# Next weights turned by VectorE in 32x32 blocks, loads that exchange partition groups, and a contraction index dealt with a stride of four

## The chip, the cores and the metric

The kernel runs on one core of one Trainium2 chip. The metric is the device time of one execution in microseconds (us); three runs of the kernel before have a median of 3421.34 us (3419.98 to 3421.66). The engines are TensorE (PE; its weight loads are listed as PEld), VectorE (DVE), ScalarE (ACT), GpSimd (POOL) and SyncE (SP, which here only issues DMAs).

## The reference

All tensors are f32; 128 sequences of 32 tokens with 512 channels (4096 tokens).

1. Conditional mixing: a small MLP on `cond_128` gives each sequence a 32x32 matrix and a bias, with which its 32 rows are mixed.
2. A Mamba-like block of 8 groups: `proj = h @ in_proj_w.T` (in_proj_w has 10304 rows of 512), a causal convolution of 4 taps with SiLU, a scan per head (`state = state*dA + dt*x*B; y = state.C`), a norm per group of 512 channels, a gate, and `out = yn @ out_proj_w.T` (out_proj_w is 512 x 4096). It is added to x.
3. A grouped convolution and a 512x512 layer whose weights are decoded from bit planes with a table of 16 or 256 entries per output row; the wide table serves rows of large norm. It is added too.

What matters for the change is only how in_proj_w and out_proj_w get into the form that TensorE wants: contraction index on the partitions, and each weight as a high part (rounded to the matmul's format) and a low part (the rest), since each f32 product is made of three passes (high.high, high.low, low.high).

## The kernel before, in words

Stage 1 (until about 113 us) makes the mixed rows h for 8 blocks of 512 tokens and stores them, high and low, in `h_d`, and turns the 14 weight chunks (128x512 each) of group 0: `turn` transposes a chunk in four 128x128 pieces on TensorE, ScalarE copies the high part from PSUM, VectorE subtracts for the low part. `mix_chunk` takes 128 columns of x (`xb`) as stationary operand for each k of the four contraction pieces.

Stage 2 is a loop over 8 groups g and, within one, 8 blocks j; `attend` is its body on every engine, run 64 times. In groups 0 to 6 it is called with `prepare`: it also prepares two chunks of the next group's weights. One body does, on TensorE in this order: six projections (`project`, 12 matmuls each, L1119) for B, C and four of x; C.B products (L1156); the decay sums (L1164); three gate projections; the transposes of xc (`turn_x`, L1126); eight 128x128 transposes of the next weights (L1181) into two banks; the scan (L1136), whose first part waits tile by tile for `dtx`; the fourth gate projection; the output product (L1211). Without `prepare` (last group) there are no such transposes and the third gate projection comes after `turn_x`.

VectorE does in this order: the convolutions (L1343) with pieces of the wide-table decode between them, four scan matrices `m` (L1361), four products `dtx` (L1368, these need `turn_x`), two low parts of the next weights (L1381, these need ScalarE's copy), then `y`, `z`, the low parts of `gy`, squares, more of the decode, and the addition to `acc` (L1438). ScalarE does the first taps (L1252), SiLU (L1234), the exponentials (L1258), gates 0 to 2 (`gate`, L1238), the two high copies of the next weights (L1269), then high parts of `gy` and squares with gate 3 between them. GpSimd makes the scan's products and the root.

SyncE issues in each body, in this order (`step`): a wait until the residual of the body before is stored, the loads of the two raw chunks (`load_raw`, one DMA of 256 KB each), the residual's load, in the last block of a group the reloads of `wt` as its projections come free, the stores of the two prepared chunks, the next h, and the residual's store. A group has 16 chunk places: place u = 0 takes the convolution and gate chunks 2 + j, place u = 1 takes chunks 0 and 1 in turn in blocks 0 to 3 and the four chunks of out_proj in blocks 4 to 7. Order between engines is by semaphores only, written out by hand.

Stage 3 (from about 3141 us) is the last layer. It isn't touched.

Of the kernel before, what the change touches and what calls it, by code (L numbers as in the profile page):

```python
# [18 lines left out]
F32 = mybir.dt.float32  # L19
# [4 lines left out]
ACT = mybir.ActivationFunctionType  # L24
# [3 lines left out]
P = 128  # L28
# [90 lines left out]
def same_line(nc, sb, name, partner):  # L119

    gap = (partner - next_place(nc)) % LINE
    if gap:
        sb(name, [P, gap // 4])


# [9 lines left out]
def mix_part(nc, a, sh, ctx):  # L135
# [98 lines left out]
    def block_at(place):  # L234

        return (place + 1) % NBLK

    def raw_chunk(n):

        if n < NPJ_ALL:  # L240
            return raw[n][:, :]
        return sh.stage[n - NPJ_ALL][:, :]
# [131 lines left out]
    def tensor_part(pe):  # L374

        def turn(n):

            pe.wait_ge(s_rawin[n], 16)
            if TURN_AFTER[n]:
                if TURN_AFTER[n] > NPJ_ALL:  # L380
                    pe.wait_ge(sh.s_wot, 16 * (TURN_AFTER[n] - NPJ_ALL))
                else:
                    pe.wait_ge(sh.s_wt[TURN_AFTER[n] - 1], 16)
            for k in range(KC):
                ins = pe.transpose(sh.bank[TURN[n]][:, k * P:(k + 1) * P], raw_chunk(n)[:, k * P:(k + 1) * P], sh.ident[:, :])
            ins.then_inc(s_wps, 1)
# [50 lines left out]
        def mix_chunk(j, k, alone=False):  # L437

            for t in range(TT):
                ins = pe.matmul(p_h[k][:, t * P:(t + 1) * P], xb[j % 2][:, t, k * P:(k + 1) * P], mix[:, TT * block_at(j) + t, :],  # L440
                                start=(alone and t == 0), stop=(not alone and t == TT - 1), skip_group_check=True)
            if not alone:
                ins.then_inc(s_hp, 1)
# [37 lines left out]
        for k in range(KC):  # L481
            ins = pe.transpose(p_wdt[:, k * H:(k + 1) * H], wdt[:, k * P:(k + 1) * P], sh.ident[0:H, 0:H])
        ins.then_inc(s_pe, 1)
# [372 lines left out]
def attend_part(nc, a, sh, ctx):  # L856
# [39 lines left out]
    bank = sh.bank  # L896
    XT, SEG, CB, YB, OUT, SSQ, NEXT = (3, 4, 5, 7), (5, 7), 6, (6, 7, 4, 5), (2, 3, 4, 5), 6, (0, 1)

    s_raw = [sem(f"s2_raw{u}") for u in range(2)]
    s_nps = sem("s2_nps")
    s_nhi = sem("s2_nhi")
# [69 lines left out]
    def sync_part(sp):  # L973
# [9 lines left out]
        def load_raw(g, j):  # L983
            for u, n in enumerate(next_chunks(j)):
                sp.dma_start(stage[u][:, :], weight_rows(a, n, g)).then_inc(s_raw[u], 16)

# [123 lines left out]
    def tensor_part(pe):  # L1110
        def attend(g, j, prepare):
# [50 lines left out]
            for q in range(SEGB):  # L1162
# [4 lines left out]
                ins.then_inc(s_seg, 1)  # L1167
            for c in range(CT - 1 if prepare else CT - 2):
                pe.wait_ge(s_conv, NCV * it + 4 + c)
                project(NCV + c)  # L1170
# [5 lines left out]

            for u in range(2 if prepare else 0):
                pe.wait_ge(s_raw[u], 16 * it + 16)
                pe.wait_ge(s_z, CT * it + CT + 1 + u)
                for k in range(KC):  # L1180
                    ins = pe.transpose(bank[NEXT[u]][:, k * P:(k + 1) * P], stage[u][:, k * P:(k + 1) * P], sh.ident[:, :])  # L1181
                ins.then_inc(s_nps, 1)
            if not prepare:
                pe.wait_ge(s_conv, NCV * it + NCV)
                project(NCV + CT - 2)
            pe.wait_ge(s_cbm, it + 1)
# [3 lines left out]
            pe.wait_ge(s_z, CT * it + CT + 1)  # L1190
            if prepare:
                pe.wait_ge(s_nlo, 2 * it + 1)
            project(NCV + CT - 1)

            pe.wait_ge(s_z, CT * it + CT + 3)
            if prepare:
                pe.wait_ge(s_nlo, 2 * it + 2)
            for c in range(CT):
# [29 lines left out]
    def scalar_part(act):  # L1228
        def attend(g, j, prepare, first=False):
# [36 lines left out]
            for u in range(2 if prepare else 0):  # L1266
                act.wait_ge(s_nps, 2 * it + u + 1)
                act.wait_ge(s_nst, 32 * it + 32)
                act.activation(wnext[:, u, 0, :], bank[NEXT[u]][:, :], ACT.Copy).then_inc(s_nhi, 1)  # L1269
            high(0)  # L1270
# [19 lines left out]
    def vector_part(dve):  # L1290
        lut8 = sh.lut8[:, :, :].rearrange("p t c -> p (t c)").bitcast(I32)
        la, lb, lc, ld = (x[:, :] for x in leaf)
        def attend(wt_tile, gl, j, prepare, first=False):
            g = G // OT * wt_tile + gl
# [79 lines left out]
            for t in range(TT):  # L1374
                scan_matrix(t)
            for t in range(TT):
                times_dt(t)

            for u in range(2 if prepare else 0):
                dve.wait_ge(s_nhi, 2 * it + u + 1)  # L1380
                dve.tensor_tensor(wnext[:, u, 1, :], bank[NEXT[u]][:, :], wnext[:, u, 0, :].bitcast(F32),  # L1381
                                  ALU.subtract).then_inc(s_nlo, 1)
# [57 lines left out]

        with dve.Fori(0, NBLK) as j:
            attend(0, 0, j, True, first=True)
        with dve.Fori(0, NBLK) as j:
            attend(0, 1, j, True)
        for wt_tile in range(1, OT):
            with dve.Fori(0, G // OT - (wt_tile == OT - 1)) as gl:
                with dve.Fori(0, NBLK) as j:
                    attend(wt_tile, gl, j, True)
        with dve.Fori(0, NBLK) as j:
# [444 lines left out]
```

## Time and profile before

| | us |
|---|---|
| median of three runs | 3421.34 |
| the profiled execution's own time | 3419.63 |
| its span, first to last instruction | 3417.9 |
| PE busy | 3395.8 |
| DVE busy | 3025.9 |
| ACT busy | 1406.9 |
| POOL busy | 446.0 |
| mean granted TensorE clock | 0.999 |

Busy time is the time in which at least one instruction of the engine is under way; waits, semaphore work and DMA issues aren't in it. The queues' mean busy share of the 16 DMA engines is 38.8%. The time of a kernel is taken from its own runs; the profile is one execution, whose length differs a little.

### The profile page before, as it was taken

How to read it: one execution, taken by the hardware profiler on the slowest of the kernel's cores; microseconds unless marked ns; L12 is line 12 of the kernel's file. 1: busy time of each engine (PE TensorE's matmuls, PEld its weight loads, DVE VectorE, ACT ScalarE, POOL GpSimd, SP SyncE). 2: the span in 40 equal slices, each digit the busy share in tenths (PEclk: the TensorE clock that was granted, in tenths of full speed). 3: DMA queues.
4: the chain of work that ended last, by engine and by line, in shares of the span. 5: the costliest groups of instructions: out<-in, count | busy, mean ns of one | idle time of the engine just before them, and what ended most of it. 6: DMA issues, size and time to landing. Idle time of an engine off the chain costs nothing. (4 is left out here: it accounts for less than half of the span.)

```text
span 3417.9 us, 58378 instructions
## 1 busy us (share of the span) xinstructions
PE 3395.8 (99%) x19738; PEld 2869.8 (84%) x19738; DVE 3025.9 (89%) x4815; ACT 1406.9 (41%) x2179; POOL 446.0 (13%) x328
## 2 busy tenths in 40 slices
PE   8999999999999999999999999999999999999999
PEld 6788888888888888888888888888888888888888
DVE  6899999999999999999999999999999999998443
ACT  5555553444434444344443444434444334433111
POOL 1111111011110111101111011110111100111333
PEclk9999999999999999999999999999999999999999
DMA  7433263234432353325433262335423352225331
GB/s 270 172 117 123 105 226 132 107 135 161 159 130 109 135 191 128 131 108 191 136 128 132 107 221 106 127 132 181 148 106 127 131 181 94 76 95 154 93 92 59
DMA packets 207789, 466.23 MB, mean 136 GB/s; under 512 B 35134, under 2 KB 80606, under 8 KB 198284
## 3 DMA queue, kind: packets, MB, share of 16 engines
q1 hardware_dynamic: 206364, 464.72, 38.8%
q0 software_dynamic: 368, 0.85, 0.1%
q10 hardware_dynamic: 1024, 0.27, 0.0%
q8 instruction: 15, 0.25, 0.0%
q14 instruction: 18, 0.15, 0.0%
HBM read 313.68 MB, written 152.09 MB: 136 GB/s over the span
## 5 line engine op out<-in xcount | busy, mean ns | idle before, releaser
L1119 PE MATMUL p_cv<-ht,wt 128*128 128x512 f32 x5376 | 1274.5, 392 | 0.8 <-DVE xc L1343 0.8
L1119 PEld LDWEIGHTS p_cv<-ht,wt 128*128 128x128 f32 x5376 | 1004.0, 188 | 224.3 <-issue 11.0
L1211 PE MATMUL bank<-wot,gy 128*128 128x512 f32 x3072 | 728.3, 392 | 0.0
L1211 PEld LDWEIGHTS bank<-wot,gy 128*128 128x128 f32 x3072 | 571.9, 188 | 121.0
L1252 ACT ACTIVATE xc<-p_cv,cvb,cvw 128x512 f32<-128x512 f32 x256 | 200.0, 782 | 898.6 <-PE p_cv L1119 898.4
L1343 DVE SCALAR_TENSOR_TENSOR xc<-p_cv,cvw,xc 128x496 f32<-128x496 f32 (+2 forms) x768 | 545.0, 717 | 22.1 <-ACT xc L1252 0.2
L1119 PE MATMUL bank<-ht,wt 128*128 128x512 f32 x2304 | 554.6, 390 | 0.0
L1119 PEld LDWEIGHTS bank<-ht,wt 128*128 128x128 f32 x2304 | 431.9, 188 | 89.3
L1071 POOL TENSOR_TENSOR r<-rv,neg_half 128x4 f32<-128x4 f32 x64 | 89.5, 1398 | 2345.0 <-DVE rv L1423 2345.0
L1065 POOL TENSOR_TENSOR segr<-adts,mask_le 128x1024 fp32r<-128x1024 f32 x128 | 243.0, 1920 | 424.0 <-DVE adts L1326 424.0
L1361 DVE TENSOR_TENSOR m<-cbm,y 128x1024 f32<-128x1024 f32 x256 | 295.9, 1218 | 0.0
L1343 DVE SCALAR_TENSOR_TENSOR xc<-bank,cvw,xc 128x496 f32<-128x496 f32 (+2 forms) x384 | 274.5, 715 | 11.2 <-ACT xc L1252 2.2
L1234 ACT ACTIVATE xc<-xc 128x512 f32<-128x512 f32 x384 | 234.5, 627 | 65.2 <-DVE xc L1343 64.0
L1242 ACT ACTIVATE gy<-z 128x512 fp32r<-128x512 f32 x256 | 161.3, 630 | 212.2 <-DVE z L1397 212.2
L1136 PE MATMUL bank<-m,dtx 128*64 128x128 f32 x4096 | 237.7, 274 | 0.0
L1136 PEld LDWEIGHTS bank<-m,dtx 128*64 128x64 f32 x4096 | 222.3, 137 | 12.2 <-issue 12.2
L1368 DVE TENSOR_TENSOR dtx<-bank,dt_all 128x512 f32<-128x512 f32 x256 | 160.4, 684 | 74.3 <-PE bank L1126 74.3
L1397 DVE SCALAR_TENSOR_TENSOR z<-z,nw,y 128x512 f32<-128x512 f32 x256 | 192.4, 752 | 29.8 <-DVE y L1393 5.7
L1393 DVE SCALAR_TENSOR_TENSOR y<-xc,dsk,bank 128x512 f32<-128x512 f32 x256 | 189.6, 741 | 10.4 <-PE bank L1136 10.4
L1685 PE MATMUL p_y<-wq,x3t 128*128 128x512 f32 x768 | 182.9, 394 | 0.0
L1386 DVE TENSOR_TENSOR gy<-z,gy 128x512 fp32r<-128x512 f32 x256 | 175.2, 684 | 0.0
L1438 DVE SCALAR_TENSOR_TENSOR acc<-bank,r,acc 128x512 f32<-128x512 f32 x256 | 173.6, 740 | 0.0
(191 smaller groups left out, 3418.1 us busy)
## 6 DMA issues: line engine op xcount, KB each, us to landing
ht<-h_d SPq DMA_DIRECT2D x63, 2048.0 KB, 7.9
acc_d<-acc SPq DMA_DIRECT2D x64, 1024.0 KB, 4.3
wt_d<-wnext SPq DMA_DIRECT2D x112, 512.0 KB, 3.4
acc<-acc_d SPq DMA_DIRECT2D x56, 1024.0 KB, 7.1
wt<-wt_d SPq DMA_DIRECT2D x70, 512.0 KB, 8.4
stage<-in_L_attn_in_proj_w SPq DMA_DIRECT2D x84, 256.0 KB, 2.8
wot<-wt_d SPq DMA_DIRECT2D x28, 512.0 KB, 6.4
xb<-in_x SPq DMA_DIRECT2D x8, 1024.0 KB, 8.3
```

The lines of the kernel that those rows point to most:

```text
L1065: pool.tensor_tensor(segr[:, half, :, :], adts[:, half, :].bitcast(F32).unsqueeze(2).to_broadcast([P, TT * HG, L]), sh.mask_le[:, :].unsqu ...
L1119: ins = pe.matmul(pb[:, :], wt[:, n, l, k, :], ht[:, rr, k, :], start=(q == 0 and k == 0), stop=(q == 2 and k == KC - 1))
L1136: ins = pe.matmul(bank[YB[c]][u * HP:(u + 1) * HP, t * P:(t + 1) * P], dtx[:, t, h * HP:(h + 1) * HP], m[:, h, t, :], start=True, stop=True)
L1211: ins = pe.matmul(bank[OUT[t]][:, :], gy[:, c, l, t * P:(t + 1) * P], wot[:, rr, c, :], start=(c == 0 and q == 0), stop=(c == CT - 1 and q ...
L1234: act.activation(xc[:, n, :], xc[:, n, :], ACT.Silu).then_inc(s_silu, 1)
L1252: act.activation(xc[:, n, :], bank[PROJ_BANK[n]][:, :], ACT.Identity, bias=cvb[:, n:n + 1], scale=cvw[:, n, TAPS - 1:TAPS]).then_inc(s_tap, 1)
L1343: ins = dve.scalar_tensor_tensor(dst, src, cvw[:, n, TAPS - 1 - k:TAPS - k], dst, ALU.mult, ALU.add)
L1361: dve.tensor_tensor(m[:, :, t, :].rearrange("p h (c l) -> p h c l", l=L), cbm[:, t, :].rearrange("p (c l) -> p c l", l=L).unsqueeze(1).to_ ...
L1386: dve.tensor_tensor(gy[:, c, 1, :], z[:, c, :], gy[:, c, 0, :].bitcast(F32), ALU.subtract).then_inc(s_ulo, 1)
L1393: dve.scalar_tensor_tensor(y[:, c, :], xc[:, 2 + c, :], dsk[:, c:c + 1], bank[YB[c]][:, :], ALU.mult, ALU.add).then_inc(s_y, 1)
L1397: dve.scalar_tensor_tensor(z[:, c, :], z[:, c, :], nw[:, c:c + 1], y[:, c, :], ALU.mult, ALU.mult).then_inc(s_u, 1)
L1685: ins = pe.matmul(p_y[t % 2][q][:, :], x3t[:, l, t, r, :], wq[:, q, rr, r, :], start=(n == 0 and r == 0), stop=(n == 2 and r == R - 1))
```

## The change

Three parts, which need each other.

1. In stage 2 the next weights are no longer transposed by TensorE. VectorE's `transpose` turns 32x32 blocks each in its place; the exchange of the blocks themselves is done by the loads, which put each square of 32 rows on another group of 32 partitions. A chunk of in_proj is loaded by four DMAs (pieces of 512 bytes), a chunk of out_proj by sixteen (pieces of 128 bytes), the last four of them behind a wait for the first twelve. VectorE's transpose stands after the scan matrices and ahead of `dtx` and writes to where the low part will be; ScalarE's high copy and VectorE's low part then read it from SBUF.
2. For in_proj the contraction index is dealt with a stride of four: piece k holds channels k, k+4, k+8, ... in place of 128 neighbours, so the block transpose reads every fourth word of its source. The first group's weights, x in `mix_chunk` and the dt weights follow (`inner_columns`). The chunks of out_proj keep their order; for them the source is read without a step, and since that is another instruction, VectorE's loops over j are cut into blocks 0 to 3 and 4 to 7.
3. TensorE's order with `prepare` becomes the one without: two gate projections, `turn_x`, the third, the scan, the fourth; its waits for the low parts of the next weights go.

```diff
+def inner_columns(src, k):
+    return src.rearrange("p (q c) -> p c q", c=KC)[:, k, :]
...
             for k in range(KC):
-                ins = pe.transpose(sh.bank[TURN[n]][:, k * P:(k + 1) * P], raw_chunk(n)[:, k * P:(k + 1) * P], sh.ident[:, :])
+                columns = inner_columns(raw_chunk(n), k) if n < NPJ_ALL else raw_chunk(n)[:, k * P:(k + 1) * P]
+                ins = pe.transpose(sh.bank[TURN[n]][:, k * P:(k + 1) * P], columns, sh.ident[:, :])
...
-                ins = pe.matmul(p_h[k][:, t * P:(t + 1) * P], xb[j % 2][:, t, k * P:(k + 1) * P], mix[:, TT * block_at(j) + t, :],
+                ins = pe.matmul(p_h[k][:, t * P:(t + 1) * P], inner_columns(xb[j % 2][:, t, :], k), mix[:, TT * block_at(j) + t, :],
...
-            ins = pe.transpose(p_wdt[:, k * H:(k + 1) * H], wdt[:, k * P:(k + 1) * P], sh.ident[0:H, 0:H])
+            ins = pe.transpose(p_wdt[:, k * H:(k + 1) * H], inner_columns(wdt[:, :], k), sh.ident[0:H, 0:H])
...
         def load_raw(g, j):
             for u, n in enumerate(next_chunks(j)):
-                sp.dma_start(stage[u][:, :], weight_rows(a, n, g)).then_inc(s_raw[u], 16)
+                src = weight_rows(a, n, g)
+                for m in range(P // L):
+                    if n < NPJ:
+                        sp.dma_start(stage[u][m * L:(m + 1) * L, :].rearrange("p (m x) -> p m x", x=P),
+                                     src[:, m * P:(m + 1) * P].rearrange("(m p) x -> p m x", p=L)).then_inc(s_raw[u], 16)
+                        continue
+                    parts = src[m * L:(m + 1) * L, :].rearrange("p (c b e) -> b p c e", c=KC, e=L)
+                    if m == P // L - 1:
+                        sp.wait_ge(s_rawout, 16 * (P // L - 1) * (P // L) * (KC * (g - 1) + j - (NBLK - KC) + 1))
+                    for b in range(P // L):
+                        sp.dma_start(stage[u][b * L:(b + 1) * L, m * P:(m + 1) * P].rearrange("p (c e) -> p c e", e=L),
+                                     parts[b]).then_inc(s_rawout if m < P // L - 1 else s_raw[u], 16)
...
-            for c in range(CT - 1 if prepare else CT - 2):
+            for c in range(CT - 2):
                 pe.wait_ge(s_conv, NCV * it + 4 + c)
                 project(NCV + c)
...
-            for u in range(2 if prepare else 0):
-                pe.wait_ge(s_raw[u], 16 * it + 16)
-                pe.wait_ge(s_z, CT * it + CT + 1 + u)
-                for k in range(KC):
-                    ins = pe.transpose(bank[NEXT[u]][:, k * P:(k + 1) * P], stage[u][:, k * P:(k + 1) * P], sh.ident[:, :])
-                ins.then_inc(s_nps, 1)
-            if not prepare:
-                pe.wait_ge(s_conv, NCV * it + NCV)
-                project(NCV + CT - 2)
+            project(NCV + CT - 2)
...
             pe.wait_ge(s_z, CT * it + CT + 1)
-            if prepare:
-                pe.wait_ge(s_nlo, 2 * it + 1)
             project(NCV + CT - 1)
             pe.wait_ge(s_z, CT * it + CT + 3)
-            if prepare:
-                pe.wait_ge(s_nlo, 2 * it + 2)
...
                 act.wait_ge(s_nps, 2 * it + u + 1)
-                act.wait_ge(s_nst, 32 * it + 32)
-                act.activation(wnext[:, u, 0, :], bank[NEXT[u]][:, :], ACT.Copy).then_inc(s_nhi, 1)
+                act.activation(wnext[:, u, 0, :], wnext[:, u, 1, :].bitcast(F32), ACT.Copy).then_inc(s_nhi, 1)
...
+            if prepare:
+                dve.wait_ge(s_nst, 32 * it + 32)
+            for u in range(2 if prepare else 0):
+                dve.wait_ge(s_raw[u], 16 * (P // L) * it + 16 * (P // L))
+                dve.transpose(wnext[:, u, 1, :].bitcast(F32).rearrange("p (k m e) -> p m k e", k=KC, e=L),
+                              stage[u][:, :].rearrange("p (m k e) -> p m k e" if u == 1 and out_rows else "p (m e k) -> p m k e",
+                                                       k=KC, e=L)).then_inc(s_nps, 1)
             for t in range(TT):
                 times_dt(t)
...
-                dve.tensor_tensor(wnext[:, u, 1, :], bank[NEXT[u]][:, :], wnext[:, u, 0, :].bitcast(F32),
+                dve.tensor_tensor(wnext[:, u, 1, :], wnext[:, u, 1, :].bitcast(F32), wnext[:, u, 0, :].bitcast(F32),
                                   ALU.subtract).then_inc(s_nlo, 1)
...
+        HALVES = ((0, NBLK - KC, False), (NBLK - KC, NBLK, True))
+        for lo, hi, out_rows in HALVES:
+            with dve.Fori(lo, hi) as j:
+                attend(0, 0, j, True, first=True, out_rows=out_rows)
...
```

## Rows read from the trace of the kernel before

**Rows 1.** The page, part 1: busy us (share of the span) xinstructions.

```profile
PE 3395.8 (99%) x19738; PEld 2869.8 (84%) x19738; DVE 3025.9 (89%) x4815; ACT 1406.9 (41%) x2179; POOL 446.0 (13%) x328
```

**Rows 2.** Windows over one body of group 3 and one of the last group.

```profile
1502.16:1549.61 47.45, 47.45 (x278) 40.14 (x276) 44.48 (x71) 19.75 (x31) 5.22 (x3) 1.00 0.34 120
3016.69:3063.27 46.58, 46.58 (x269) 39.16 (x268) 43.27 (x69) 18.55 (x29) 5.20 (x3) 1.00 0.24 90
```

**Rows 3.** Waits: who waited for whom, us in total, times, longest.

```profile
DVE dtx L1368 <- PE bank L1126: 74.3, 56, 1.3
...
DVE z L1397 <- DVE y L1393: 5.7, 24, 0.5
```

**Rows 4.** Timeline of TensorE, bodies as in rows 2: start, length, what.

```profile
1509.43 2.89 PE L1119 MATMUL bank<-ht,wt 128*128 128x512 f32 x12
...
1513.90 1.04 PE L1181 MATMUL p_cv<-ident,stage 128*128 128x128 f32 x8
1514.86 3.71 PE L1136 MATMUL bank<-m,dtx 128*64 128x128 f32 x64
...
1533.24 5.65 PE L1119 MATMUL p_cv<-ht,wt 128*128 128x512 f32 x24
...
3023.97 1.91 PE L1126 MATMUL bank<-ident,xc 128*128 128x128 f32 x16
```

**Rows 5.** Timeline of VectorE in the body of group 3.

```profile
1506.83 4.63 DVE L1361 TENSOR_TENSOR m<-cbm,y 128x1024 f32<-128x1024 f32 x4
1512.79 2.53 DVE L1368 TENSOR_TENSOR dtx<-bank,dt_all 128x512 f32<-128x512 f32 x4 [1.33 <-PE bank L1126]
1515.25 1.29 DVE L1381 TENSOR_TENSOR wnext<-p_cv,wnext 128x512 fp32r<-128x512 f32 x2
1516.45 0.74 DVE L1393 SCALAR_TENSOR_TENSOR y<-xc,dsk,bank 128x512 f32<-128x512 f32 x1
```

**Rows 6.** Timeline of ScalarE in the same two bodies.

```profile
1506.85 1.16 ACT L1234 ACTIVATE xc<-xc 128x512 f32<-128x512 f32 x2
...
1514.62 1.09 ACT L1269 ACTIVATE wnext<-p_cv 128x512 fp32r<-128x512 f32 x2 [1.67 <-PE p_cv L1181]
...
3028.64 0.60 ACT L1238 ACTIVATE z<-bank 128x512 f32<-128x512 f32 x1 [3.88 <-PE bank L1119]
```

**Rows 7.** Groups of instructions (busy us, mean ns of one), and a timeline row of L730.

```profile
L730 DVE STREAM_TRANSPOSE turned<-p_cv 128x512 f32<-128x512 f32 x2 | 1.3, 694 | 1.9 <-PE p_cv L420 1.9
L687 DVE TENSOR_SCALAR bits<-bits 128x512 int32<-128x512 int32 x3 | 1.1, 422 | 0.0
...
18.15 1.31 DVE L730 STREAM_TRANSPOSE turned<-p_cv 128x512 f32<-128x512 f32 x2 [1.87 <-PE p_cv L420]
```

**Rows 8.** Groups with strided operands, one plain load (L1126), and the mix timeline.

```profile
L261 DVE COPY mix<-turned 32x256 f32<-32x256 f32 x4 | 1.5, 378 | 0.1
L270 ACT ACTIVATE mix<-turned 32x256 f32<-32x256 f32 x4 | 2.6, 653 | 4.9 <-DVE turned L730 4.9
L1279 ACT ACTIVATE acc<-z 128x512 f32<-128x512 f32 x32 | 33.6, 1126 | 42.7 <-DMA z<-in_x 42.7
L1753 DVE TENSOR_REDUCE sqs<-sq 128x128 f32<-128x512 f32 x32 | 34.9, 1091 | 40.6 <-ACT sq L1713 40.6
L1126 PEld LDWEIGHTS bank<-ident,xc 128*128 128x128 f32 x1024 | 115.6, 140 | 8.4
L1662 PEld LDWEIGHTS p_y<-ident,w 128*128 128x128 f32 x12 | 1.7, 209 | 0.2 <-DVE wq L1736 0.2
...
90.37 2.05 PE L440 MATMUL p_cv<-mix,xb 128*128 128x128 f32 x16
```

**Rows 9.** SyncE's timeline; the landing of L1596's loads; an issue row (KB, landing).

```profile
1542.06 0.35 SPq L985 DMA_DIRECT2D stage<-in_L_attn_in_proj_w  x1
...
3168.89 4.49 SPq L1596 DMA_DIRECT2D x2p<-acc_d  x8
...
DMA to landing us min/median/max: 2.4/3.2/4.2
...
cvw<-in_L_attn_conv_weight SPq DMA_DIRECT2D x8, 8.0 KB, 2.9
```

More of the change, by code:

```diff
@@ L896, in attend_part @@
     bank = sh.bank
-    XT, SEG, CB, YB, OUT, SSQ, NEXT = (3, 4, 5, 7), (5, 7), 6, (6, 7, 4, 5), (2, 3, 4, 5), 6, (0, 1)
+    XT, SEG, CB, YB, OUT, SSQ = (3, 4, 5, 7), (5, 7), 6, (6, 7, 4, 5), (2, 3, 4, 5), 6
     s_raw = [sem(f"s2_raw{u}") for u in range(2)]
+    s_rawout = sem("s2_raw_out_parts")
     s_nps = sem("s2_nps")
@@ L1292, in vector_part, with attend @@
         la, lb, lc, ld = (x[:, :] for x in leaf)
-        def attend(wt_tile, gl, j, prepare, first=False):
+        def attend(wt_tile, gl, j, prepare, first=False, out_rows=False):
             g = G // OT * wt_tile + gl
@@ L1439, in attend @@
                                          ALU.mult, ALU.add).then_inc(s_acc, 1)
[L1441 to L1444, printed above, removed]
+        HALVES = ((0, NBLK - KC, False), (NBLK - KC, NBLK, True))
+        for lo, hi, out_rows in HALVES:
+            with dve.Fori(lo, hi) as j:
+                attend(0, 0, j, True, first=True, out_rows=out_rows)
+        for lo, hi, out_rows in HALVES:
+            with dve.Fori(lo, hi) as j:
+                attend(0, 1, j, True, out_rows=out_rows)
         for wt_tile in range(1, OT):
             with dve.Fori(0, G // OT - (wt_tile == OT - 1)) as gl:
-                with dve.Fori(0, NBLK) as j:
-                    attend(wt_tile, gl, j, True)
+                for lo, hi, out_rows in HALVES:
+                    with dve.Fori(lo, hi) as j:
+                        attend(wt_tile, gl, j, True, out_rows=out_rows)
         with dve.Fori(0, NBLK) as j:
```

## The prediction

> **What bounds the kernel now.** I read the page first: TensorE (PE) is busy 99% of the span, VectorE 89% [rows 1]. Most of the span is one body run 64 times (8 groups of 8 blocks), so next I cut one body out of the middle by windows: 47.45 us with `prepare`, in which PE is busy for all 47.45; one of the last group, without `prepare`, takes 46.58, again with PE busy throughout, and the granted clock is 1.00 in both [rows 2]. The sums of busy time understate VectorE, because its short gaps between dependent instructions count as idle, so I read the waits instead: in the 56 prepared bodies VectorE waits for another engine in one place only, 74.3/56 = 1.33 us before the `dtx` products, for TensorE's transposes of xc [rows 3]. VectorE's own loop is then 47.45 - 1.33 = 46.12 us. So TensorE is the bound, and VectorE is 1.33 us behind it; whatever VectorE gets beyond that is on the path.
>
> **The change, step by step.**
>
> *TensorE loses the eight transposes of the next weights.* They start at 1513.90 and the scan follows at 1514.86: 0.96 us [rows 4]. What is left, order included (transposes of xc ahead of the third gate projection), is the stream that the last group runs already. Its 46.58 us is the new floor of TensorE: 0.87 less. If nothing else held, 56 x 0.87 = 49 us would go. The last group also shows that the new order is harmless to PE: the transposes of xc need the last silu, which ends at 1506.85 + 1.16 = 1508.01, and PE would reach them at 1509.43 [rows 4, 6].
>
> *VectorE gains two 32x32-block transposes of 128x512 per body,* ahead of `dtx`. The one transpose in the trace, twice 128x512 from PSUM in stage 1, takes 694 ns, and the two together 1.31, so the second starts 0.62 after the first [rows 7]. The new ones read SBUF, which makes no difference: the scan matrices, all from SBUF, run 4 x 1024 elements in 4.63, 1.13 ns each, and a low part that reads PSUM has a pitch of 0.60 for 512 (the instruction after the pair starts 1.20 after the first, by the chain of [rows 5]: 1515.25 to 1516.45), 1.17 ns each. But 84 of the 112 read with a step of four words (16 bytes), which no VectorE row shows. Bounds: below, a 1-input instruction of the same size at 422 ns (pitch 0.34 by the same overlap) [rows 7]; above, the strided sum over `sq` at 1091 ns (pitch 1.02). ScalarE's strided copy `acc<-z`, with exactly this step of 16 bytes, is at 1126 ns [rows 8] where its plain copy takes 0.60 [rows 6], so a strided read can cost 1.9 times. The nearest row for VectorE is a copy whose read steps 128 bytes: 256 elements in 378 ns, while ScalarE takes 653 for the same kind of copy of the same size [rows 8]. 378 ns is about one element per cycle of 1.04 ns plus 0.11, no worse than its unit-step instructions; the `sq` row is a reduction over runs of four, which may be slow for that alone. I take 0.62 for each transpose, strided or not.
> The row `acc<-z` shows ScalarE paying for a 16-byte step. The Trainium skill, "SBUF — State Buffer", section "Door 1: The DMA port swizzle", says that SBUF delivers in lines of 16 bytes and wants at least two hits per line for full rate; taken at its word, a step of four f32 has one hit, and the strided transposes cost what the first rival below says. The VectorE copy in rows 8 speaks against it for this engine.
>
> *What the cover is worth.* VectorE ends the scan matrices at 1506.83 + 4.63 = 1511.46 and idles until 1512.79 [rows 5]. Now it transposes there (from 1511.39, since an instruction overlaps the one before by 0.07), and the transposes of xc, 2.7 us earlier on PE, are done before it gets to `dtx`. New loop of VectorE: 46.12 + 2 x 0.62 = 47.36 us, above PE's 46.58. The wait on TensorE is gone; what is late next is VectorE itself, and TensorE waits for it (at the scan, for the fourth `dtx`, about 0.8 us). Net: 47.36 - 47.45 = -0.09 per body, 56 x -0.09 = **-5.0 us**.
>
> *ScalarE's high copy and VectorE's low part* keep their count and size. The copy now stands behind the third gate, whose projection moved behind the transposes of xc. In the last group this gate starts 3028.64 - 3023.97 = 4.67 after those transposes start [rows 4, 6]. With them at 1509.43 or 0.16 earlier (`dtx` can start at 1511.39 + 1.24 = 1512.63 in place of 1512.79, and PE's lead comes from there) the gate starts near 1514.0, the copies (a pair spans 1.09: pitch 0.49, length 0.60) end near 1515.1 and 1515.6. VectorE wants its low parts at 1511.39 + 1.24 + 4 x 0.61 = 1515.1 and 1515.7. It fits with about 0.1 to spare: I charge 0 and keep up to 0.3 per body for the range. Queued behind a late low part are the `y`, `z` and square steps, so it would be on the bound's path.
>
> *SyncE's loads.* Two issues per body become 8 in blocks 0 to 3 and 20, with a wait for twelve landings in the middle, in blocks 4 to 7. The first issue is at 1542.06, once the residual is stored [rows 9]. Eight issues to a quarter of the partitions, with register work, take 4.49, 0.56 each, and such a load lands in 3.2 us (2.4 to 4.2) [rows 9]. In the long case the sixteenth is issued at 1542.06 + 15 x 0.56 = 1550.5, lands at 1553.6, the last four are out at 1555.3 and land at 1558.5. VectorE wants chunk 0 at 1511.39 + 47.36 = 1558.75 and chunk 1, the one loaded so, at 1559.4. Margin 0.9 us: cost 0, up to 1 us in each of 28 bodies if both landings are at the 4.2 end. Behind them in the queue stand the residual's load, some 12 us later then and wanted only at the block's end, and in the last block of a group nine reloads of `wt`, which go out from about 1556 on and are wanted one after the other from the next block's start, 25 us later (1533.24 + 47.45 = 1580.7, by the first projection of the block shown) [rows 4]. The store of the prepared weights and the load of ht follow events of the compute engines later than that. Cost 0. DMA traffic: same bytes, pieces of 512 or 128 bytes; 512 pieces of 16 bytes (8 KB of `cvw`) land in 2.9 us [rows 9].
>
> *VectorE's loops are cut in halves.* One more loop start for each of 7 group passes. The trace's few starts of a gap that belong to no engine (`z` behind `y`, 5.7 us in 24 cases, 0.5 at most) [rows 3] bound it: 0 to 4, I take +1.
>
> *Stage 1 reads x and the first weights with the step of four.* 256 matmuls of `mix` and 44 transposes load strided operands. Plain transposes load in 140 ns, those of stage 3 with this very step in 209 [rows 8]. Loads overlap the matmuls: 16 of `mix` take 2.05, 0.128 each [rows 8], less than one plain load, so most of the 69 ns should hide. Bounds 0 and 256 x 0.069 = 18 us; I take +1.
>
> **Sum:** -5.0 + 1 + 1 = -3 us on the profiled execution's 3419.63. The median of the runs is 1.7 above that, 3421.34, so the time to forecast is **3418 us**. What a measurement here can tell from no change is 0.2%, 6.8 us; this is within it.
>
> **Rivals.**
> 1. *VectorE pays for the 16-byte step* (the other side). Place: the 84 strided transposes, pitch 1.02 in place of 0.62. Blocks 0 to 3: 46.12 + 2.04 = 48.16, +0.71 x 28 = 19.9; blocks 4 to 7, where chunk 1 of out_proj is read plainly: 46.12 + 1.64 = 47.76, +0.31 x 28 = 8.7. With the +2 above: 3421.3 + 30.6 = 3452. It decides from a mean pitch of 0.665 per transpose on (1.33/2). For: ScalarE, PE loads and the reduction in rows 8. Against: the VectorE copy there.
> 2. *The high copy comes late,* 0.3 us per body: loop 47.66, +0.21 x 56 = 12, time 3421.3 + 12 + 2 = 3435. For: the margin of 0.1; against: PE has 0.8 us of slack to run ahead.
> 3. *The raw rows come late in blocks 4 to 7,* by 1 us: +28 - 3, time 3446. Against: the margin of 0.9. The Trainium skill, "DMA: Bandwidth & Descriptors", "Specifications", wants 512 bytes per piece for line rate, with a read-modify-write below; at that the 128-byte pieces would be this rival. The row of 16-byte pieces speaks for a landing of about 3 us all the same.
> 4. *Transposes are cheap,* pitch 0.34: loop 46.80, -0.65 x 56 + 2 = -34, time 3387. For: 422 ns for a 1-input instruction; against: 694 ns for the transpose itself.
> 5. *PE's lost work is not what held it* (a reload or the clock takes its place) and nothing moves: 3421. Against: no wait of PE in the bodies.
>
> **How the numbers follow.** Forecast 0.61, rival 1 0.17, rival 2 0.08, rival 3 0.05, rival 4 0.05, rival 5 0.04. The forecast's own range, with a pitch of 0.59 to 0.66 and the +2 between 0 and 8, is 3412 to 3428: of its 0.61 I give 0.17 to faster than 3414.5, 0.39 to within, 0.05 to slower than 3428. Faster 0.17 + 0.05 = 0.22. Same 0.39 + 0.04 + 0.01 (a mild rival 2) = 0.44. Slower 0.05 + 0.17 + 0.07 + 0.05 = 0.34. The range goes from 3409 to 3452: it leaves out rival 4, the forecast's tail below and half of rival 1.
>
> **What would show it.** Body period 47.3 to 47.4 in groups 0 to 6 and 46.58 in the last. STREAM_TRANSPOSE in the body at 0.69 us in both patterns; 1.09 in the strided one means rival 1. No wait before `dtx`; PE idle 0.8 per body before the scan for `dtx`. A VectorE wait before `wnext` for ACT means rival 2, one before the transpose for DMA of `stage` rival 3. LDWEIGHTS of `mix` near 0.21, stage 1 ending within 2 us of before. I am wrong at the root if VectorE has waits left in the body while PE is idle: then a loop over two engines sets the period, which I haven't summed.

## The result and the profile after

| | before | after |
|---|---|---|
| median, us (four runs each) | 3421.15 | 3456.93 |
| lowest to highest | 3419.98 to 3421.66 | 3456.59 to 3457.55 |
| span of the profiled execution | 3417.9 | 3455.8 |

After takes 1.0105 times as long as before [1.0088, 1.0123]: slower by 1%, 39 us above the 3418 forecast and 5 above the end of the range.

The page of after, part 1 (columns as in rows 1):

```profile
PE 3415.6 (99%) x19290; PEld 2844.2 (82%) x19290; DVE 3113.7 (90%) x4927; ACT 1404.7 (41%) x2179; POOL 445.5 (13%) x328
```

PE issues 448 matmuls fewer (8 in each of 56 bodies) and is busy 20 us longer. The matmuls of `mix` alone are busy 64.4 us, 36.8 before; and a matmul that is held up counts as busy: the scan's 4096 matmuls, unchanged, are busy 270.1 us (L1154), 237.7 before (L1136). As in [rows 1], 99% doesn't say that PE's own work is what takes the time.

I laid the spans side by side at one mark of each body, the start of VectorE's product for C.B. The first such mark stands at 127.13 us before and 150.47 after; from there the distances from mark to mark are:

| | before | after | count | together, us |
|---|---|---|---|---|
| until the first mark | 127.13 | 150.47 | 1 | +23.3 |
| blocks 0 to 3, groups 0 to 6 | 47.46 | 47.77 | 28 | +8.7 |
| blocks 4 to 7, groups 0 to 6 | 47.46 | 47.41 | 28 | -1.4 |
| on top, one body between two groups (54.33) | | | 1 | +6.9 |
| last group | 46.58 | 46.58 | 8 | 0 |

The sum is 37.5 of the 37.9 us between the spans. The first line is good to a few us only: over the profiles of the versions with after's stage 1 (after, e3, e4, e7 to e9) the first mark stands between 149.1 and 153.7, over those with the stage 1 of before (before, e5, e6, e10 to e12) between 127.1 and 129.1. Here are the rows for each line.

*Stage 1.* After's groups for the matmuls of `mix` and their loads, and PE's timeline, the same sixteen as in [rows 8]:

```profile
L446 PE MATMUL bank<-mix,xb 128*128 128x128 f32 x128 | 32.5, 424 | 1.1 <-ACT mix L275 1.1
L446 PEld LDWEIGHTS bank<-mix,xb 128*128 128x128 f32 x128 | 30.5, 329 | 4.3 <-issue 4.3
L446 PEld LDWEIGHTS p_cv<-mix,xb 128*128 128x128 f32 x128 | 30.5, 329 | 2.6 <-issue 2.6
...
94.83 4.00 PE L446 MATMUL p_cv<-mix,xb 128*128 128x128 f32 x16
```

Sixteen took 2.05 us [rows 8] and take 4.00: 0.25 each. A load that steps 16 bytes takes 329 ns.

*The bodies.* Windows over a body of blocks 0 to 3 and one of blocks 4 to 7 (as in [rows 2]; the first is 0.03 longer than a period):

```profile
1436.00:1483.80 47.80, 47.35 (x271) 39.16 (x270) 46.17 (x73) 19.72 (x32) 5.19 (x3) 1.00 0.28 99
1483.90:1531.30 47.40, 47.08 (x270) 39.09 (x269) 45.79 (x72) 19.69 (x31) 5.19 (x3) 1.00 0.36 122
```

PE is now idle 0.45 and 0.32 us in them, where it was busy throughout. VectorE's timeline in the first, and its two instructions after the same place in the second:

```profile
1439.82 4.62 DVE L1366 TENSOR_TENSOR m<-cbm,y 128x1024 f32<-128x1024 f32 x4
1444.36 2.04 DVE L1385 STREAM_TRANSPOSE wnext<-stage 128x512 f32<-128x512 f32 x2
1446.34 2.43 DVE L1373 TENSOR_TENSOR dtx<-bank,dt_all 128x512 f32<-128x512 f32 x4
1448.69 1.28 DVE L1393 TENSOR_TENSOR wnext<-wnext 128x512 fp32r<-128x512 f32 x2
1449.90 0.73 DVE L1405 SCALAR_TENSOR_TENSOR y<-xc,dsk,bank 128x512 f32<-128x512 f32 x1
...
1492.14 1.67 DVE L1385 STREAM_TRANSPOSE wnext<-stage 128x512 f32<-128x512 f32 x2
1493.73 2.44 DVE L1373 TENSOR_TENSOR dtx<-bank,dt_all 128x512 f32<-128x512 f32 x4
```

The chain `m`, transposes, `dtx`, low parts, `y` has no gap: the wait of [rows 5] is gone and nothing took its place. Two strided transposes take the engine 1446.34 - 1444.36 = 1.98 us, one strided and one plain 1.59. One line of the listing by source gives all 112 (shortest, median, longest), and the waits show who stands behind VectorE:

```profile
L1385 DVE STREAM_TRANSPOSE wnext<-stage x112: 665/1059/1080, 158.6 to 2784.5; 128x512 f32<-128x512 f32 x112
```

```profile
PEld bank L1154 <- DVE dtx L1373: 53.4, 140, 0.4
...
PE bank L1154 <- DVE dtx L1373: 18.2, 113, 0.4
```

*The one long body.* VectorE's timeline where group 4 turns into group 5 (groups counted from 0):

```profile
2038.59 2.72 DVE L1450 SCALAR_TENSOR_TENSOR acc<-bank,r,acc 128x512 f32<-128x512 f32 x4
2047.29 0.19 DVE L1325 TENSOR_TENSOR adt<-dt_all,neg_a 128x32 f32 x1 [5.98 <-issue]
```

VectorE stands 5.98 us with nothing that the profile shows to wait for.

### The profile page after: what moved, and what is told of

Its sections match the earlier page's. It is cut to its first block and busy times, and to the rows that moved or that the text cites. A ratio compares the mean times of both kernels' runs of the same rounds, so it can differ in the third digit from the quotient of the medians.

```text
span 3455.8 us, 59237 instructions
## 1 busy us (share of the span) xinstructions
PE 3415.6 (99%) x19290; PEld 2844.2 (82%) x19290; DVE 3113.7 (90%) x4927; ACT 1404.7 (41%) x2179; POOL 445.5 (13%) x328
## 5 line engine op out<-in xcount | busy, mean ns | idle before, releaser
L1154 PE MATMUL bank<-m,dtx 128*64 128x128 f32 x4096 | 270.1, 278 | 21.7 <-DVE dtx L1373 18.2
L1154 PEld LDWEIGHTS bank<-m,dtx 128*64 128x64 f32 x4096 | 219.6, 136 | 81.3 <-DVE dtx L1373 53.4
L1308 DVE TENSOR_SCALAR leaf<-mask,lut 128x512 int32<-128x512 int32 x320 | 166.9, 539 | 0.0
```

The source lines that it names most:

```text
L1154: ins = pe.matmul(bank[YB[c]][u * HP:(u + 1) * HP, t * P:(t + 1) * P], dtx[:, t, h * HP:(h + 1) * HP], m[:, h, t, :], start=True, stop=True)
```

## The experiments

Each ratio is against the kernel before, run beside it on the same chip; the medians of before were 3420.2, 3421.29, 3421.34 and 3421.37 us in four sittings.

### Stage 1 alone: e1 and e2

e1 is after with the `mix` matmuls reading neighbouring columns; it leaves the order of the channels of h wrong against that of the weights.

```diff
-                ins = pe.matmul(..., inner_columns(xb[j % 2][:, t, :], k), mix[...],
+                ins = pe.matmul(..., xb[j % 2][:, t, k * P:(k + 1) * P], mix[...],
```

> The changed kernel with x read plainly again by the stage 1 matmuls (128 neighbouring columns as stationary operand); its h then has another channel order than the weights. Theory A (the strided weight loads of x are what stage 1 lost): a load of mix goes back from 329 to 192 ns, 16 of these matmuls from 4.00 to 2.05 us, the first cbm product of stage 2 comes at 127 to 129 us in place of 150.5, and the time falls by 21 to 24 us to about 3434. Rival B (the strided transposes of the first weights and the dt weights shift the hand-overs of stage 1): the first cbm stays above 140 and the time falls by less than 12 us.

Measured: 3435.59 us, ratio 1.0045 [1.0028, 1.0062]; first mark 127.34; the bodies as in after, with a long one of 54.94. e2 is before with only that read made strided, so with the opposite mismatch.

> The kernel before with nothing but x read with a step of four words as stationary operand of the stage 1 matmuls (h in another channel order than the weights). Theory A: the load goes from 192 to 329 ns, stage 2 starts 21 to 24 us later, bodies stay at 47.46, time 3421 + 22 = 3443. Rival B: under 12 us more.

Measured: 3443.97 us, 1.0068 [1.0051, 1.0085]; first mark 151.32, bodies 47.46. PE's timeline and loads of e1, the plain ones:

```profile
57.92 2.05 PE L446 MATMUL p_cv<-mix,xb 128*128 128x128 f32 x16
...
L446 PEld LDWEIGHTS p_cv<-mix,xb 128*128 128x128 f32 x128 | 15.7, 200 | 2.6 <-issue 2.6
```

The edit gives 21.3 us back when taken out of after and costs 23.8 when put into before. So the 256 strided operands of `mix` are nearly all of stage 1's 23 us; the strided transposes of the first weights, which e1 keeps, leave its first mark at 127.34, where before has 127.13.

### The transposes with plain reads, and one loop: e3 and e4

e3 is after with both chunks read without a step (in_proj's columns then land in the wrong order); e4 is e3 with VectorE's loop over j in one piece.

```diff
-    stage[u][:, :].rearrange("p (m k e) -> p m k e" if u == 1 and out_rows else "p (m e k) -> p m k e",
+    stage[u][:, :].rearrange("p (m k e) -> p m k e",
...
-        HALVES = ((0, NBLK - KC, False), (NBLK - KC, NBLK, True))
+        HALVES = ((0, NBLK, False),)
```

> The changed kernel with both VectorE transposes reading their source without a step in all blocks; what lands in the high and low parts of the in_proj weights is another order of the same words. Theory A (VectorE alone sets the body, 45.8 us of its own work and the two transposes): a transpose at 1059 ns becomes 670 everywhere, bodies of blocks 0 to 3 go from 47.77 to 47.0, those of blocks 4 to 7 from 47.41 to 47.0; time -28 x 0.77 - 28 x 0.4 = -33, about 3424. Rival B (a loop over TensorE, ScalarE and VectorE, by the third gate moved behind the transposes of xc and the scan's wait for dtx, holds the body near 47.4): bodies stay at 47.3 to 47.45, time about 3446.

> As the experiment with plain reads in all blocks, and VectorE's loops over the blocks of a group in one piece again instead of halves (possible since both halves are now the same instruction). Theory A: the single body of 54.3 us in group 5, with VectorE idle for 6.0 us with nothing it waited for, comes from the doubled loop code; in one loop no such body appears, and the time is 5 to 8 us below that experiment if it has one there, equal if it has none. Rival B: the gap is of one execution and has nothing to do with the loops: it appears or not in either, and the times agree within 2 us.

Measured: e3 3437.03 us, 1.0047 [1.003, 1.0064], bodies 47.16 with one of 55.57; e4 3426.33, 1.0018 [1.0009, 1.0028], bodies 47.16 and none above 47.49. e3's transposes by source line, then its waits:

```profile
L1385 DVE STREAM_TRANSPOSE wnext<-stage x112: 665/686/707, 160.5 to 2764.2; 128x512 f32<-128x512 f32 x112
```

```profile
DVE wnext L1393 <- ACT wnext L1274: 12.0, 55, 0.2
...
DVE adt L1325 <- issue: 6.1, 1, 6.1
```

The same transposes read plainly take 686 ns in place of 1059: the step costs that, as rival 1 said. The one loop takes the stall of 6.1 us away; it is 10.7 us faster than e3. In the two profiles 8.4 of that is the long body and 1.8 lies ahead of the first mark (152.39 in e3, 150.56 in e4), in stage 1, which the edit doesn't touch: about 8 us can be put down to the loop. But the bodies stop at 47.16, not at the 47.0 that VectorE's own work alone would give: its low parts now wait for ScalarE's copy (12.0 us in 55 bodies; e4's listing has the same line). Theory A of e3 had 47.0 and 3424; the stall and this wait are most of what it missed.

### What the step costs VectorE: e6

e6 is before with eleven instructions of VectorE more at the end of stage 2, each on a piece of 128x512 but for the last, on 32x512. Each was run once and each row is one instruction; the words are f32. The edit, abridged, with the line numbers put beside it:

```diff
+        dve.transpose(y[:, 1, :], flat[0])                                        # L1455 step 1; 1456 to 1458: 2, 4, 16
+        dve.transpose(z[:, 1, :].rearrange("p (x e k) -> p x k e", x=4, k=4), ...)  # L1459 writes with a step of 4
+        dve.tensor_copy(z[:, 2, :], flat[1])                                      # L1460 step 1; 1461, 1462: 4, 16
+        dve.tensor_tensor(..., flat[2] with a step of 4, flat[1], ALU.add)         # L1463
+        dve.tensor_copy(..., step of 2); dve.tensor_copy(..., 32 partitions, 16)    # L1465, L1466
```

> The kernel before with eleven VectorE instructions at the end of stage 2 on data nobody uses: block transposes of 128x512 reading with a step of 1, 2, 4 and 16 words and one writing with a step of 4; copies reading with a step of 1, 2, 4 and 16, an addition of which one source steps by 4, and a copy by 16 on 32 partitions. Theory A (every VectorE read whose step is 16 bytes or more pays, at 1.8 ns per element): transposes with steps 4 and 16 near 1.06 us, with 1 and 2 near 0.68; copies with steps 4 and 16 near 1.06; the copy on 32 partitions pays too. Rival B (the stage 1 copy with a step of 128 bytes was free, so only the transpose pays): copies 0.69 or less with every step. Rival C: the cost grows with the step from 2 words on.

Measured, by source line (shortest, median and longest are one value, since each ran once):

```profile
L1455 DVE STREAM_TRANSPOSE y<-xc x1: 703/703/703, 3144.8 to 3144.8; 128x512 f32<-128x512 f32 x1
L1456 DVE STREAM_TRANSPOSE y<-xc x1: 671/671/671, 3145.5 to 3145.5; 128x512 f32<-128x512 f32 x1
L1457 DVE STREAM_TRANSPOSE y<-xc x1: 1046/1046/1046, 3146.1 to 3146.1; 128x512 f32<-128x512 f32 x1
L1458 DVE STREAM_TRANSPOSE z<-xc x1: 995/995/995, 3147.0 to 3147.0; 128x512 f32<-128x512 f32 x1
L1459 DVE STREAM_TRANSPOSE z<-xc x1: 1046/1046/1046, 3147.9 to 3147.9; 128x512 f32<-128x512 f32 x1
L1460 DVE COPY z<-xc x1: 413/413/413, 3148.8 to 3148.8; 128x512 f32<-128x512 f32 x1
L1461 DVE COPY z<-xc x1: 591/591/591, 3149.2 to 3149.2; 128x512 f32<-128x512 f32 x1
L1463 DVE TENSOR_TENSOR dtx<-xc x1: 1044/1044/1044, 3150.2 to 3150.2; 128x512 f32<-128x512 f32 x1
L1465 DVE COPY dtx<-xc x1: 417/417/417, 3151.1 to 3151.1; 128x512 f32<-128x512 f32 x1
```

The step of 16 words in a copy is L1462, shown at the end with L1466. A step of two words (8 bytes) costs nothing, a step of four costs 343 ns per 512 elements in a transpose (1046 - 703), read or written, and a step of 16, tried as a read only, costs no more than one of four. A plain copy takes 413 ns and a copy with a step of four 591. That is the error in my evidence: I compared a strided *copy* with unit-step instructions of another kind, which take 1.7 times as long as a copy (703). The copy pays too, though less than theory A had (591, not 1060). It starts from a faster plain rate.

The Trainium skill, "SBUF — State Buffer", "Door 1: The DMA port swizzle", wants two hits in each line of 16 bytes. These rows agree: two f32 of a line are used at a step of two (671), one at a step of four (1046). The rule I weighed and set aside in the prediction was the right one. The same passage gives four f32 as the step that is still free; measured here, a step of two is and one of four isn't.

### The step in the write: e5

e5 keeps the contraction's plain order everywhere, deals the *rows* of a chunk by four, and writes the transposes with the step; its loop over j is in one piece. Of the edit, the write:

```diff
+                dve.transpose(wnext[:, u, 1, :].bitcast(F32).rearrange("p (k e m) -> p m k e", k=KC, e=L), ...
```

> A version with the step on the write side: stage 1 as before; the contraction index in its plain order; a chunk's rows are dealt with a stride of four over the squares instead, so that VectorE's transpose reads plainly and writes every fourth word; in_proj chunks by four DMAs and out_proj chunks by sixteen, all in pieces of 128 bytes; VectorE's loops in one piece. It computes the reference. Theory A: a write with a step costs VectorE nothing, as the bit extraction of stage 1 (it writes every eighth word, 698 ns for 512 elements) has the rate of one element per cycle: transposes at 0.68, bodies at 47.0, stage 1 as before: 3421 - 56 x 0.46 = 3395. Rival B: it costs what the read costs, 1059 ns: bodies 47.8, time 3421 + 56 x 0.33 = 3440. Rival C: the raw rows in 128-byte pieces come late: a wait of VectorE for the stage tile.

Measured: 3434.96 us, 1.0041 [1.0027, 1.0055]; first mark 128.72; bodies 47.66, the last of a group 48.0 to 48.6 from group 1 on (why is open); its transposes, 112 of them:

```profile
L1387 DVE STREAM_TRANSPOSE wnext<-stage 128x512 f32<-128x512 f32 x112 | 111.3, 1069 | 0.0
```

Stage 1 is repaired; the write with a step costs VectorE what the read did, now in all 112. The row from which theory A took a free write, the bit extraction at 698 ns, was no evidence for it: a plain instruction of the same kind and size, though a shift alone, takes 422 [rows 7].

### How low the loop goes: e7, e8 and e9

e7 is after with a plain copy in place of each transpose (the next weights aren't turned), to see what an even cheaper VectorE step would bring.

```diff
-                dve.transpose(wnext[:, u, 1, :].bitcast(F32).rearrange(...), stage[u][:, :].rearrange(...)).then_inc(s_nps, 1)
+                dve.tensor_copy(wnext[:, u, 1, :].bitcast(F32), stage[u][:, :]).then_inc(s_nps, 1)
```

> The changed kernel with a plain copy of 128x512 in place of each VectorE transpose (the next weights aren't turned). Theory A (VectorE's own work sets the body; TensorE's floor is 46.58): a copy at 0.4 us gives 45.8 + 0.7 = 46.5 for VectorE, so the body falls to TensorE's 46.6 in groups 0 to 6 and VectorE shows a wait again; time 3457 - 28 x (47.77 - 46.6) - 28 x (47.41 - 46.6) = 3401. If the copy runs at one element per cycle (0.68): bodies 47.0, time 3424. Rival B (a loop over several engines): bodies stay above 47.2.

Measured: 3434.82 us, 1.0041 [1.0025, 1.0056]; the copies take 419 ns, the bodies 47.13, one is 54.65; neither the 46.6 of theory A nor rival B's 47.2 and more. VectorE has 2 x (0.686 - 0.419) = 0.53 us less to do than in e3, and the period fell by 0.03. ScalarE's and VectorE's timelines in a body, and the waits:

```profile
1481.09 0.60 ACT L1244 ACTIVATE z<-bank 128x512 f32<-128x512 f32 x1 [3.88 <-PE bank L1137]
1481.58 1.14 ACT L1274 ACTIVATE wnext<-wnext 128x512 fp32r<-128x512 f32 x2
...
1482.24 1.29 DVE L1391 TENSOR_TENSOR wnext<-wnext 128x512 fp32r<-128x512 f32 x2 [0.74 <-ACT wnext L1274]
...
1489.99 6.40 PE L1217 MATMUL bank<-wot,gy 128*128 128x512 f32 x27 [0.27 <-DVE y L1403]
```

```profile
DVE wnext L1391 <- ACT wnext L1274: 40.9, 56, 0.7
...
PE bank L1217 <- DVE y L1403: 15.3, 55, 0.4
```

This is a loop over three engines: PE's third gate projection, ScalarE's gate and the high copy behind it, VectorE's low parts and all queued behind them (`y`), PE's output product. It sets 47.13 with PE and VectorE both idle in it.

e8 is e4 with ScalarE's two high copies put ahead of the third gate; e9 is e7 with one loop and the same move.

```diff
+            (the two high copies of the next weights)
             gate(2)
-            (the two high copies of the next weights)
```

> As the experiment with plain reads in all blocks and one loop (bodies 47.16, VectorE waits 12.0 us in 55 bodies for ScalarE's high copy), with ScalarE's two high copies ahead of its third gate in place of behind it. Theory A (a loop over three engines adds to VectorE's own work there: transposes of xc, third gate projection, third gate, high copy, low part, y, output product): the wait is gone, bodies at VectorE's own 46.95 to 47.0, time 10 us lower than that experiment, about 3416 to 3417. Rival B (the copy is late because ScalarE is late by itself): the wait stays, bodies 47.16.

> As the experiment with a plain copy in place of each transpose (bodies 47.13, VectorE waits 40.9 us for the high copy, TensorE 15.3 us for y), with the high copies ahead of the third gate and VectorE's loops in one piece. Theory A (TensorE's floor is 46.58 once the loop over three engines is open): bodies 46.6 in all groups, time 3434.8 - 56 x 0.53 - 7 = 3398. Rival B (some other wait of TensorE holds 47.13): bodies stay above 47.

Measured: e8 3420.81 us, 0.9998 [0.9989, 1.0008], bodies 47.01 to 47.07, and no wait of VectorE for ScalarE before the low parts; the time is 4 us above theory A. e9 3394.69 us, 0.9921 [0.9906, 0.9936], 46.58 to 46.59 in all groups but for a start of 46.53 and one of 46.73. A window of e9 over one period:

```profile
1436.00:1482.58 46.58, 46.58 (x270) 39.16 (x269) 44.93 (x73) 19.82 (x31) 5.20 (x3) 1.00 0.36 124
```

So the floor of 46.58 that I gave PE is right, and both its conditions are needed: the copies early, and VectorE with less than that to do.

### Versions that compute the whole result: e10, e11 and e12

With plain reads the pair of transposes fits VectorE only almost, so e10 gives each engine one: the in_proj chunk of place 0 stays with PE (four transposes ahead of the third gate projection), place 1 goes to VectorE by sixteen loads of 128-byte pieces, the copies stand early, stage 1 and the contraction are as before, and there is one loop. e11 gives both to VectorE, with 32 loads per body, issued a body ahead behind the load of h except in group 0 and in the first block of each group, where they stay at the body's own start. e12 is e10 with one move on SyncE:

```diff
+            (load_raw of this body)
             sp.wait_ge(s_accst, 16 * it + 16)
-            (load_raw of this body)
```

> A version that computes the reference and shares the turning: the chunk u = 0 is transposed by TensorE as before (four transposes, ahead of the third gate projection, one plain load), the chunk u = 1 by VectorE with plain reads (sixteen loads in 128-byte pieces), high copies ahead of the third gate, contraction index in plain order, stage 1 as before, VectorE's loops in one piece. Theory A: TensorE 46.58 + 0.48 = 47.06, VectorE 45.8 + 0.6 = 46.4 by itself; body 47.06 to 47.1, time 3421 - 56 x 0.38 = 3400. Rival B: a loop over several engines, or late rows, keeps the body at 47.2 or more.

> A version that computes the reference with both chunks turned by VectorE with plain reads: every chunk loaded by sixteen DMAs in 128-byte pieces, issued behind the load of h one body ahead (in group 0 and in each first block still at the start of the body), high copies ahead of the third gate, stage 1 as before, loops in one piece. Theory A: VectorE's own work sets the body, 45.8 + 1.2 = 47.0; time 3421 - 56 x 0.46 = 3395, and a few us more where 32 issues at 0.49 us come late (8 bodies of group 0, one per group later, up to 1.5 us each, so 3395 to 3412). Rival B: the residual's store, now behind the issues, delays the next body: bodies of blocks 1 to 7 above 47.2.

> The version that shares the turning (TensorE the chunk u = 0, VectorE the chunk u = 1), with the raw loads of a body issued ahead of SyncE's wait for the residual's store in place of behind it (they don't need it), some 4 us earlier. There the first body of each group was 48.6 to 51.0 long, with VectorE waiting up to 3.0 us for the raw rows. Theory A: the rows are then in time, the first bodies come to 47.05 as the others, time 3410.7 - 15 = 3396 to 3400. Rival B: the issues themselves are slow there (0.77 us each behind the reloads of a new group) and share the queue with the store, so less than half of the 15 us comes back, time 3404 or more.

| | us | ratio to before | bodies | the first body of a group |
|---|---|---|---|---|
| e10 | 3410.66 | 0.997 [0.9958, 0.9982] | 47.05 | 48.6 to 51.0 |
| e11 | 3511.49 | 1.0264 [1.025, 1.0278] | 47.02 to 47.07 | 60 to 65 |
| e12 | 3403.08 | 0.9947 [0.9933, 0.9961] | 47.05 | 47.1 to 48.5 |

e12 is faster than both kernels. The move on SyncE gives back 7.6 of the 15 us, between what its theory A and its rival B said; e10 is 11 us above the 3400 of its theory A, by the first bodies alone. The window of e12 over one period shows PE busy throughout again, with four transposes (0.47 us) on top of the floor:

```profile
1436.00:1483.05 47.05, 47.05 (x273) 39.60 (x273) 45.08 (x72) 19.66 (x31) 5.21 (x4) 1.00 0.37 123
```

What is left is in the first bodies (47.1 to 48.5 for 47.05), where the sixteen loads come out behind the reloads of `wt` and `wot`. SyncE's timeline of e12 there, and its and e11's longest waits for raw rows:

```profile
487.91 5.80 SPq L1057 DMA_DIRECT2D wot<-wt_d  x4
493.75 1.73 SPq L1060 DMA_DIRECT2D acc_d<-acc  x1
495.79 0.80 SPq L994 DMA_DIRECT2D stage<-in_L_attn_in_proj_w  x1
496.81 12.53 SPq L999 DMA_DIRECT2D stage<-in_L_attn_in_proj_w  x16
```

```profile
DVE wnext L1391 <- DMA stage<-in_L_attn_in_proj_w: 7.4, 5, 2.0
```

```profile
DVE wnext L1381 <- DMA stage<-in_L_attn_in_proj_w: 89.3, 15, 11.4
```

The first of the two waits is e12's (14.4, 6, 3.0 in e10), the second e11's. With twice the loads it is 6 to 12 times as long in sum, and e11 loses by it all that it might win, with group 0 at 47 to 53 us a body. Its long waits stand only where the 32 loads are issued at the body's own start; the bodies whose loads are issued one body ahead run at 47.02 to 47.07. A second queue for the loads wasn't tried.

## Why the prediction was wrong, step by step

- **What bounds the kernel before: right.** PE's floor without the eight transposes is 46.58 (e9), and VectorE is the bound of the changed kernel: no wait before `dtx`, PE idle in front of the scan. Rival 5 is out with it: with the transposes off PE, VectorE's part cheap and the copies early, the body does fall to 46.58.
- **Stage 1, the costliest error.** I charged +1 with an upper bound of 18; it measured +23.3 in the marks, 21.3 and 23.8 in e1 and e2. Both failed. The 69 ns of a strided load came from [rows 8], transposes in stage 3; the `mix` loads grew from 200 (e1) to 329, by 129. And "most of the 69 ns should hide" is false: sixteen matmuls went from 2.05 to 4.00, 0.122 more each, about the load's own growth. Over all 256 PE was busy 27.6 us longer (64.4 - 36.8) for the 23.3 of stage 1. I read it so: where loads follow each other at 0.128 us, the loads are the pace, and most of what is added to one is added to the time.
- **The transposes: rival 1's mechanism, at a quarter of its price (+7.3 us, not 28.6).** I took 0.62 for a strided one; it is 0.99. Rival 1 said 1.02, but 48.16 and 47.76 per body; measured are 47.77 and 47.41. The term off there is VectorE's own work: 47.77 - 1.98 = 45.79 and 47.41 - 1.59 = 45.82, not 46.12. A wait that the profile lists as 1.33 us gave back 1.6. From the timelines, the four `dtx` products ran at 2.35 in place of 2.46 (they had followed PE's transposes one by one), the first convolutions of a later tap had about 0.1 of gaps hidden as well, and 0.07 is the overlap of an instruction that needn't wait. Blocks 0 to 3 thus cost +8.7 us rather than 19.9, and blocks 4 to 7 gained 1.4. The range ends at 3452 because of this rival; that the time came within 5 us of it is luck, since what the rival had too much (28.6 - 7.3) is about what stage 1 had too little (23.3 - 1).
- **The loops in halves: +1 foreseen, bounds 0 to 4; measured +6.9,** in one of the seven passes. It is in after, e1, e3 and e7, which have VectorE's bodies twice, and in none of those that have them once (e4, e5, e8 to e12). e3 against e4, where nothing else differs, shows that doubling the loop's code brings it; why in that one pass and no other is open. That it is the fetch of that code is not shown, but the traces' DMA records point there: in each of the four, two 8 KB transfers of the kind "instruction" fall into the stall (in after at 2043.38 and 2043.92, the stall being 2041.31 to 2047.29), and e4, e5 and e8 to e12 have none in the 12 us ahead of VectorE's start in that place.
- **The high copy: charged 0, kept to 0.3 for the range (rival 2).** In after it costs nothing, since VectorE is later still. It was there all the same, behind the first limit: with plain transposes VectorE waits 0.2 for it in each body (e3), and it holds the loop at 47.13 to 47.16 even when VectorE has another 0.53 us less to do (e7).
- **Loads: right.** No wait of VectorE for raw rows in after, rival 3 is out. SyncE's sixteen issues take 9.55 us in the middle of a group, 0.60 each with the wait in them, and 0.56 was taken. They land 1.7 us later, not 3.2, so the margin was wider than the 0.9 I gave.
- **"Wrong at the root if a loop over two engines sets the period":** not in after. In e3 and e7 a loop over three does, and I hadn't summed it.

Rival 4's price for a cheap transpose is what a plain copy takes (419 ns, e7); no transpose does. Taken with the measured sizes, my sum gives -5.0 becoming +7.3 for the bodies, +6.9 for the loops and +23.3 for stage 1: 37.5.

## What to carry to other kernels

Before a layout is dealt with a step so that one instruction needs no shuffle, price *every* reader of that layout, the once-only stage too: here most of the loss came from an operand in stage 1 that the change touched in one expression. Judge a strided access only by the same operation at unit step, since a fast instruction with a step can look like a slow one without. When work is moved off a full engine, the time won is not that engine's freed time but the distance to the next limit, and that can be a loop over several engines: make the moved step nearly free once (as in e7 and e9) and see which period is left.

## What the runs showed of the hardware

- A stationary f32 operand of 128x128, read with a step of 16 bytes, loads into TensorE in 329 ns where a plain one takes 200, and 16 such matmuls take 4.00 in place of 2.05 us (e1, after).
- VectorE: a step of 8 bytes is free (671 against 703), a read with a step of 16 or 64 bytes makes a transpose of 703 ns one of 1046 or 995 (a write with 16 bytes: 1046), and a copy of 413 ns one of 591 or 573; the copy on 32 partitions pays as much as that on 128:

```profile
L1462 DVE COPY dtx<-xc x1: 573/573/573, 3149.7 to 3149.7; 128x512 f32<-128x512 f32 x1
...
L1466 DVE COPY dtx<-xc x1: 571/571/571, 3151.4 to 3151.4; 32x512 f32<-32x512 f32 x1
```

- The issue of a 16 KB load costs SyncE more for in_proj than for out_proj, in the same shape (128 bytes a piece): 564 against 317 ns, register work not counted. It goes with the source, not with the place in the group: in one body of e11 sixteen from in_proj take 12.50 us and the sixteen from out_proj behind them 7.95; in e12 it is 11.3 to 12.5 in each of blocks 0 to 3 and 9.1 in blocks 4 to 7. Why is open. e12, by source line (shortest, median, longest), then after:

```profile
L999 SPq DMA_DIRECT2D stage<-in_L_attn_in_proj_w x448: 563/564/1139, 114.6 to 2531.6; - x150
L999 SPq DMA_DIRECT2D stage<-in_L_attn_out_proj_w x448: 316/317/1144, 304.4 to 2717.8; - x150
...
1477.51 9.55 SPq L1002 DMA_DIRECT2D stage<-in_L_attn_out_proj_w  x16
```

- Such a load from out_proj lands 1.7 us after its issue (after; KB each, median us), sooner than the 3.2 us I took from other loads:

```profile
stage<-in_L_attn_out_proj_w SPq DMA_DIRECT2D x448, 16.0 KB, 1.7
```
